# A gated cross-attention and feed-forward kernel: the order of the opening

## The chip, the cores and the metric

The kernel runs on one core of one Trainium2 chip. The metric is device microseconds of that core for one launch; lower is better. Three runs of the kernel before gave 1178.39, 1178.43 and 1180.54 us, so its median is 1178.43 us. A profiled execution of its own took 1179.06 us, and 1177.3 us of that is the span from the first instruction to the last.

The core has five engines that run their own instruction streams and meet only at semaphores: TensorE (PE; its weight loads are listed apart as PEld), VectorE (DVE), ScalarE (ACT), GpSimd (POOL) and SyncE (SP), which here only issues DMAs. All loads go through the queue of SP but one of 0.5 KB, which ACT issues.

## The reference, cut to what matters

```python
# x: (8, 224, 2048), ctx: (8, 750, 512), mask: (224, 750)
x = x + tanh(g_xattn) * attention(layernorm(x), ctx, ctx, mask)   # 32 heads of 64, 8 key/value heads
x = x + tanh(g_ffn) * gated_ffn(layernorm(x), weights...)         # router, top 8 of 512 slots, gate
# attention: softmax(q @ k.T / 8 + mask) @ v, where q is layernorm(x), k = v = ctx
```

The change lies wholly in the first 25 us: in the first layer norm of batch 0 and in what leads from it to the first attention products. Everything that is computed stays as it is.

## The kernel before, in words

**Tiles.** The 224 rows of a batch are cut in two. The first 128 are the top rows, one per partition, 2048 values each, in `xa[:, b]`. The other 96 are the rest: they are laid out so that each of 128 partitions holds, for 3 blocks (`NB = 3`), a quarter of a row (512 values), in `xb[:, b % 3]`. A partition thus knows only the mean and variance of its own quarter of each rest row, and four of them have to be joined.

**Units and windows.** The attention phase walks over 64 windows (8 batches by 8 key/value heads; `GROUPS`), and each window has 7 units (`UNITS`): 4 of top rows (one for each query head of the group) and 3 of the rest. Unit `n` takes 128 query rows against 750 context rows. Its path is: scores on PE (`score_main`, line 909, 512 columns, and `score_mid`, line 920, 238 columns, each twice because the keys are split in a high and a low part), mask and maximum on DVE (line 1303, which writes `neg_max`), exponential on ACT (line 723), transposition on PE (`turn_main`, line 932, and `turn_mid`, line 939), evacuation on ACT (line 719), the low part of the split on POOL (line 590), and the value products on PE (`value`, lines 956, 957 and 962; line 962 alone needs POOL's low part). Each engine's loop has one step `k` per unit, from `FIRST = -14` on, and every stage works at its own distance: in step `k` PE turns unit `k + 2`, scores unit `k + 5` and multiplies the values of unit `k`; DVE takes the maximum of `k + 4`; ACT takes the exponential of `k + 4`; POOL splits `k + 2`. The order within a step is written out by hand, and each engine works strictly in that order.

**Keys and values.** Two sets of buffers take turns. SP loads the keys of window `w + 2` when all 7 units of window `w` are scored (`load_k`, line 412, two DMAs of 187.5 KB each, one for each half of the partitions), and the values when POOL has split the ones of window `w + 1` (`load_v`, line 415). POOL splits the keys of window `w + 2` (`split_k`, line 557) in step 5 of window `w`, ahead of the low parts of the units that follow.

**The opening.** SP issues its loads without waiting, one after the other: top rows of batch 0 (1024 KB), the rest rows (768 KB), keys 0, the first mask (375 KB), values 0, the other masks (1125 KB), keys 1, values 1, top and rest rows of batch 1, then the feed-forward weights (four times 1024 KB, 512 KB, and small ones up to `in_log_rel`). DVE runs `top_stats(0, 0..3)` (line 1174) when the top rows are there, merges them (line 1187), and then `rest_stats` (line 1181). POOL makes the scale and bias from the top rows' numbers (lines 536 to 551), ACT normalizes the first 512 columns (line 687), PE transposes two of their blocks (`turn_first(0)`, line 887), ACT rounds them to bf16 (line 703, `round_first`), DVE writes the low parts (line 1200, `split_first`), and the scores of unit 0 begin.

**The rest rows' variance** is joined by two tiny products of PE with the matrix `quad`: the mean (line 1006) and, after three small DVE steps (lines 1220 to 1224), the variance (line 1024). DVE copies the result (line 1227), and this copy stands ahead of the DVE loop and so ahead of the first maximum. It releases `rest_joined`, on which POOL waits (line 536) before it makes the factors of the rest rows and normalizes them (line 583: three pieces for `rest_first`, three for `rest_widened`). From these PE transposes the query blocks of the rest rows of pair 0: `turn_first(1)` in step -3 and `turn_first(2)` in step -2. The first unit's transposition is `turn_main(0)` in step -2, so behind `turn_first(1)` in PE's order. ACT's `round_first(1)` has the same place in step -3.

Of the kernel before, what the change touches and what calls it, by code (L numbers as in the profile page):

```python
# [20 lines left out]
NB = REST // QUAD  # L21
# [48 lines left out]
def flamingo_block(nc, x_top, x_rest, k_t, v_rows, mask, g_x, av_t, wvd_t, w1_t, wq_t, wr, wr_rows_in, keys_t, log_rel, rel, b1, w2, wvu_t,  # L70
                   scalars, spill, out):
    with ExitStack() as ctx:
# [6 lines left out]
        def sem(name):  # L79
            return ctx.enter_context(nc.semaphore(name))  # L80
# [168 lines left out]
        top_normed = sem("top_normed")  # L249
        rest_normed = sem("rest_normed")  # L250
        rest_first = sem("rest_first")
        top_second = sem("top_second")
        spilled = [sem(f"spilled{i}") for i in range(3)]
        k_loaded = [sem("k_loaded0"), sem("k_loaded1")]
# [148 lines left out]
        def _(sp):  # L403
# [3 lines left out]
            def load_top(b):  # L407
                sp.dma_start(xa[:, b, :], x_top[b]).then_inc(top_loaded[b], 16)
# [23 lines left out]
                        sp.dma_start(spill[at:at + QUAD].rearrange("i (g r d) -> i g r d", g=KV, r=REP)[:, :, r, :],  # L432
                                     xb[QUAD * r:QUAD * r + QUAD, b % 3, j].rearrange("i (g d) -> i g d", g=KV)).then_inc(spilled[b % 3], 16)

            load_top(0)
            load_rest(0)
            load_k(0)
            sp.dma_start(mask_sb[:, 0:1, :], mask[:, 0:1, :]).then_inc(mask_loaded, 16)
# [240 lines left out]
        def _(act):  # L679
# [34 lines left out]
            for k in range(FIRST, NU):  # L714
                window, m = place(k)
                n = k + 2
                if 0 <= n < NU and not evac_on_dve(n):
                    act.wait_ge(turned, n + 1)
                    act.activation(p_sb[:, n % RING, :], flat_ps[:, turned_at(n):turned_at(n) + CW], ACT.Copy).then_inc(evac_a, 1)  # L719
                n = k + 4  # L720
                if 0 <= n < NU:
                    act.wait_ge(maxed, n + 1)
                    act.activation(s_sb[:, n % RING, 0:CTX], s_sb[:, n % RING, 0:CTX], ACT.Exp, bias=neg_max[:, n % 4, :],  # L723
                                   scale=-1.0).then_inc(exped, 1)
                g = window + 1
                if m == 0 and 0 <= g < GROUPS:
                    act.wait_ge(v_loaded[g % 2], 16 * (g // 2 + 1))
                    if g >= 2:
                        act.wait_ge(valued, UNITS * (g - 1))
                    else:  # L730
                        act.wait_ge(v_ones_set, 1)
                    act.activation(v_hi[:, g % 2, :, 0:D], v_raw[:, g % 2], ACT.Copy).then_inc(v_hi_done, 1)
                pair = window // 2 + 1
                if m == 4 and 1 <= pair < PAIRS:
                    act.wait_ge(q_turned, window + 4)
                if k in (-3, -2):
                    round_first(k + 4)
                later = (window - 3) // KV + 1
                if m == 6 and window >= 1:
                    if window % KV in (1, 2):  # L740
                        norm_top(4 * (window // KV) + 1 + window % KV)
                    elif later < BATCH and window % KV == 3:
                        norm_top(4 * later)
                    elif later < BATCH and window % KV in (4, 5, 6):
                        norm_rest(later, window % KV - 4)
                    elif later < BATCH and window % KV == 7:
                        norm_top(4 * later + 1)
                if window == 2 and m == 2:
                    act.wait_ge(small_loaded, 80)
                    act.activation(tanh_gf[:, :], scal[:, 0:1], ACT.Tanh).then_inc(gf_tanh, 1)  # L750
                    act.activation(keys_hi[:, :], keys_raw, ACT.Copy, scale=float(BOT) ** -0.5).then_inc(keys_hi_done, 1)
                if window == 3 and m == 2:
                    act.wait_ge(weights_loaded, 16)
                    act.activation(wq_cat[:, :, 0:BOT], wq_raw, ACT.Copy).then_inc(wq_hi_done, 1)
                if k in (NU - 4, NU - 3):
                    round_h(0, k - (NU - 4))
# [95 lines left out]
        def _(pe):  # L852
# [154 lines left out]
            for k in range(FIRST, NU):  # L1007
                window, m = place(k)
                if 0 <= k + 2 < NU:
                    turn_main(k + 2)  # L1010
                    turn_mid(k + 2)
                if 0 <= k + 5 < NU:
                    score_main(k + 5)
                if k >= 0:
                    value(k)
                if k in (NU - 4, NU - 3):
                    turn_h(0, k - (NU - 4))
                if k == NU - 2:
                    sum_wide(0, 0)
                if 0 <= k + 5 < NU:  # L1020
                    score_mid(k + 5)
                if k + 5 == 0:
                    pe.wait_ge(own_step, 3)
                    pe.matmul(psum[:, 3, 0:NB], quad[:, :], own_sum[:, :], start=True, stop=True).then_inc(own_spread, 1)
                if m == 2 and 1 <= window // 2 + 1 < PAIRS:
                    turn_q(window)
                if k in (-3, -2):
                    turn_first(k + 4)

            def sum_v2(pieces):  # L1030
                for i in pieces:
# [134 lines left out]
        def _(dve):  # L1166
# [2 lines left out]
            dve.memset(rk_aug[:, :], 0.0).then_inc(pads_set, 1)  # L1169

            def top_stats(b, c):
                if c == 0:
                    dve.wait_ge(top_loaded[b], 16)
                ins = dve.bn_stats(stats_top[:, c, :], xa[:, b, 512 * c:512 * c + 512])
                if c == 3:
                    ins.then_inc(top_summed, 1)
# [46 lines left out]
            dve.wait_ge(own_step, 2)  # L1223
            dve.tensor_tensor(own_sum[:, :], own_sq[:, :], own_mv[:, :, 1], ALU.add).then_inc(own_step, 1)
            dve.tensor_copy(ln_mv[:, 1:1 + NB, 0], psum[:, 5, 0:NB])
            dve.wait_ge(own_spread, 1)
            dve.tensor_copy(ln_mv[:, 1:1 + NB, 1], psum[:, 3, 0:NB]).then_inc(rest_joined, 1)
            dve.wait_ge(mask_loaded, 16)
            dve.wait_ge(gx_tanh, 1)

# [65 lines left out]
            for k in range(FIRST, NU + TO_CLOSE):  # L1296
                window, m = place(k)
                n = k + 4
                if n == REP:
                    dve.wait_ge(mask_rest_loaded, 16)  # L1300
                if 0 <= n < NU:
                    dve.wait_ge(scored, n + 1)
                    dve.tensor_tensor_reduce(s_sb[:, n % RING, 0:CTX], flat_ps[:, score_at(n):score_at(n) + CTX],  # L1303
                                             mask_sb[:, max(n % UNITS - REP + 1, 0), :],
                                             -1.0, 3.4e38, ALU.add, ALU.min, neg_max[:, n % 4, :]).then_inc(maxed, 1)
                n = k + 2
                if 0 <= n < NU and evac_on_dve(n):
                    dve.wait_ge(turned, n + 1)
                    dve.tensor_copy(p_sb[:, n % RING, :], flat_ps[:, turned_at(n):turned_at(n) + CW]).then_inc(evac_v, 1)
                if m == 0 and window >= 1:  # L1310
                    add_part(window - 1, range(0, 3))
                if m == 1 and window >= 1:
                    add_part(window - 1, range(3, UNITS))
                pair = window // 2 + 1
                if m == 3 and 1 <= pair < PAIRS:
                    turns = turn_range(window)
                    dve.wait_ge(q_turned, window + 4)
                    for half in range(2):
                        dve.tensor_copy(q_t[D * half:D * half + D, pair % 2, half, turns[0]:turns[-1] + 1, :],
                                        mix_ps[D * half:D * half + D, (window + 1) % 2, 0:128 * len(turns)].rearrange("p (t n) -> p t n", n=128)  # L1320
                                        ).then_inc(q_hi_own, 1)
                if m in (4, 5) and 1 <= pair < PAIRS:
                    split_q((window + 1) % 2, pair, m - 4, turn_range(window), 2 * (window + 3) + m - 4 + 1)
                if k in (-2, -1):
                    split_first(k + 3)
                next_stats(window, m)
                b = window // KV + 1
                if 0 <= window < GROUPS and b < BATCH:
                    if window % KV == 2 and m == 2:
                        merge_top(b)  # L1330
                        merge_rest(b)
                if m == 2 and EARLY_AT <= window < EARLY_AT + 4 * EARLY:
                    u, c = divmod(window - EARLY_AT, 4)
                    if c == 0:
                        dve.wait_ge(x_added, KV * (u + 1))
                        if u >= 1:
                            dve.wait_ge(mv2_done, u)
                    bank_stats(u, c)
                    if c == 3:
                        merge2(u)  # L1340
                if k == NU - 5:
                    stage_h(0, 0)
                    stage_h(0, 1)
                if k in (NU - 3, NU - 2):
                    split_h(0, k - (NU - 3))
                    stage_h(0, k - (NU - 3) + 2)
# [221 lines left out]
```

## Time and profile before

| | us |
|---|---|
| median of three runs | 1178.43 |
| profiled execution | 1179.06 |
| its span | 1177.3 |
| PE busy | 1139.6 (97% of the span) |
| DVE busy | 944.6 (80%) |
| ACT busy | 916.7 (78%) |
| POOL busy | 889.9 (76%) |
| top rows of batch 0: issue to landing | 5.9 |
| first value product on PE begins at | 24.84 |

The profile is one execution. Its times are in us from the start of the span. The views used are the page's busy times, the chain of waits (what the last instruction was waiting for, followed back), the timeline (instructions in order of time, alike ones merged), the waits, the DMA issues with their time to landing, and busy times by stretch. A wait is put down to what ended last before it.

### The profile page before, as it was taken

What the parts mean: (1) busy time and instruction counts of PE and PEld (TensorE: products, weight loads), DVE (VectorE), ACT (ScalarE), POOL (GpSimd) and SP (SyncE); (2) the same over time, 40 slices, a digit from 0 to 9 for tenths busy, and PEclk for the clock granted to TensorE, in tenths of its full rate; (3) what the DMA queues carried; (4) which work ended last, traced back from release to release, by engine and by line L of the source; (5) the groups of instructions that cost most, each with busy time, mean ns of one, the idle gap of its engine ahead of it and who ended that gap; (6) DMA issues with size and microseconds to landing.
All of it is one profiled execution on the core that took longest, in us unless ns stands there. A gap on an engine that the chain in (4) does not pass through costs nothing.

```text
span 1177.3 us, 35064 instructions
## 1 busy us (share of the span) xinstructions
PE 1139.6 (97%) x14385; PEld 913.8 (78%) x14642; DVE 944.6 (80%) x2255; ACT 916.7 (78%) x1226; POOL 889.9 (76%) x804
## 2 busy tenths in 40 slices
PE   5999999999999999999999999999999999999997
PEld 3888888888888888888888888888887665555554
DVE  5988888888888888888888888888874899676765
ACT  5899898888998898998899988999881444555544
POOL 6899999999999999999999999999991110404222
PEclk9999999999999999999999999999999999999999
DMA  9421231132114212311321131121225500011224
GB/s 336 148 69 48 57 116 45 52 83 97 42 42 116 70 48 57 115 49 48 86 93 42 46 78 49 42 58 51 62 87 182 209 2 1 1 68 77 107 99 152
DMA packets 60735, 95.09 MB, mean 81 GB/s; under 512 B 35233, under 2 KB 44449, under 8 KB 56482
## 3 DMA queue, kind: packets, MB, share of 16 engines
q1 hardware_dynamic: 59858, 91.79, 25.4%
q8 instruction: 118, 1.93, 0.7%
q10 hardware_dynamic: 720, 1.05, 0.3%
q14 instruction: 39, 0.32, 0.1%
HBM read 71.75 MB, written 20.97 MB: 79 GB/s over the span
## 4 chain that ended last, share of the span: by engine, by line
PE 73%; POOL 20%; DMA 2%; issue 2%; DVE 2%; SPq 1%; ACT 0%; DVEq 0%; POOLq 0%
POOL arena L590 14%; PE psum L985 12%; PE psum L932 12%; PE psum L909 11%; PE psum L939 6%; PE psum L920 6%; PE psum L962 5%; PE psum L956 5%; PE psum L957 5%; PE psum L1066 3%; POOL arena L557 2%; PE psum L972 2%; PE psum L999 2%; PE psum L887 2%; POOL arena L610 1%
## 5 line engine op out<-in xcount | busy, mean ns | idle before, releaser
L590 POOL TENSOR_TENSOR arena<-arena 128x768 bf16<-128x768 f32 x448 | 651.8, 1470 | 40.2 <-ACT arena L719 37.6
L1303 DVE CUSTOM_DVE_ANT_0 arena<-psum,arena 128x750 f32<-128x750 f32 x448 | 420.5, 939 | 127.4 <-PE psum L920 121.9
L719 ACT ACTIVATE arena<-psum 128x768 f32<-128x768 f32 x448 | 362.2, 809 | 89.4 <-PE psum L939 89.3
L723 ACT ACTIVATE arena<-arena,neg_max 128x750 f32<-128x750 f32 x448 | 410.9, 917 | 3.8 <-DVE neg_max L1303 3.7
L932 PE MATMUL psum<-ident,arena 128*128 128x128 f32 x1792 | 268.8, 273 | 0.0
L956 PEld LDWEIGHTS psum<-arena 128*128 128x128 bf16 (+1 forms) x2688 | 194.7, 98 | 57.6
L909 PE MATMUL psum<-arena 128*128 128x512 bf16 x674 | 222.5, 384 | 14.9 <-DVE arena L1200 0.8
L957 PE MATMUL psum<-arena 128*128 128x64 bf16 (+1 forms) x2688 | 222.2, 193 | 0.0
L956 PE MATMUL psum<-arena 128*128 128x65 bf16 (+1 forms) x2688 | 221.9, 194 | 0.0
L957 PEld LDWEIGHTS psum<-arena 128*128 128x128 bf16 (+1 forms) x2688 | 178.5, 98 | 53.2
L932 PEld LDWEIGHTS psum<-ident,arena 128*128 128x128 f32 x1792 | 206.7, 140 | 4.3
L939 PE MATMUL psum<-ident,arena 128*128 128x128 f32 x896 | 171.5, 273 | 0.2 <-ACT arena L719 0.2
L920 PE MATMUL psum<-arena 128*128 128x238 bf16 x896 | 167.5, 268 | 0.9 <-DVE neg_max L1303 0.9
L962 PE MATMUL psum<-arena 128*128 128x65 bf16 (+1 forms) x2688 | 160.1, 194 | 1.3 <-POOL arena L590 1.3
L985 PE MATMUL psum<-arena 128*128 128x512 bf16 x648 | 156.8, 384 | 1.5
L985 PEld LDWEIGHTS psum<-arena 128*128 128x128 bf16 x672 | 63.6, 96 | 75.0 <-issue 0.8
L962 PEld LDWEIGHTS psum<-arena 128*128 128x128 bf16 (+1 forms) x2688 | 114.9, 98 | 1.9 <-POOL arena L590 1.9
L939 PEld LDWEIGHTS psum<-ident,arena 128*128 128x128 f32 x896 | 112.2, 141 | 0.5 <-ACT arena L719 0.4
L699 ACT ACTIVATE arena<-psum 128x512 bf16<-128x512 f32 x56 | 33.3, 597 | 96.2 <-PE psum L972 96.2
L1246 DVE SCALAR_TENSOR_TENSOR arena<-psum,r_den,arena 128x64 f32<-128x64 f32 x448 | 97.5, 278 | 2.3
L557 POOL TENSOR_TENSOR arena<-arena 128x750 bf16<-128x750 f32 x64 | 92.1, 1439 | 1.8 <-DMA arena<-in_k_t 1.8
L909 PEld LDWEIGHTS psum<-arena 128*128 128x128 bf16 x896 | 87.8, 98 | 6.1 <-issue 0.8
(161 smaller groups left out, 1267.1 us busy)
## 6 DMA issues: line engine op xcount, KB each, us to landing
arena<-in_k_t SPq DMA_DIRECT2D x128, 187.5 KB, 3.2
arena<-in_v_rows SPq DMA_DIRECT2D x64, 192.0 KB, 2.5
out<-arena SPq DMA_DIRECT2D x12, 1024.0 KB, 3.9
arena<-in_x_top SPq DMA_DIRECT2D x8, 1024.0 KB, 5.3
arena<-in_x_rest SPq DMA_DIRECT2D x8, 768.0 KB, 4.5
spill<-arena SPq DMA_DIRECT2D x96, 64.0 KB, 2.2
arena<-spill SPq DMA_DIRECT2D x6, 1024.0 KB, 10.6
arena<-in_w_t SPq DMA_DIRECT2D x4, 1024.0 KB, 19.9
```

The lines of the kernel that those rows point to most:

```text
L590: pool.tensor_tensor(p_lo[:, n % RING, :], p_sb[:, n % RING, :], high(p_sb[:, n % RING, :]), ALU.subtract).then_inc(p_split, 1)
L719: act.activation(p_sb[:, n % RING, :], flat_ps[:, turned_at(n):turned_at(n) + CW], ACT.Copy).then_inc(evac_a, 1)
L723: act.activation(s_sb[:, n % RING, 0:CTX], s_sb[:, n % RING, 0:CTX], ACT.Exp, bias=neg_max[:, n % 4, :], scale=-1.0).then_inc(exped, 1)
L909: pe.matmul(flat_ps[:, score_at(n) + cols.start:score_at(n) + cols.stop], q_t[:, pair % 2, half, turn, :], kk, start=(i == 0), stop=(i == 1))
L920: mm = pe.matmul(flat_ps[:, score_at(n) + cols.start:score_at(n) + cols.stop], q_t[:, g // 2 % 2, half, turn, :], kk, start=(i == 0), stop ...
L932: pe.transpose(flat_ps[:, at:at + 128], s_sb[:, n % RING, c * 128:(c + 1) * 128], ident[:, :])
L939: mm = pe.transpose(flat_ps[:, at:at + 128], s_sb[:, n % RING, c * 128:(c + 1) * 128], ident[:, :])
L956: pe.matmul(o, hi, v_hi[0:rows, u, c, :], start=(c == 0), stop=False, skip_group_check=True)
L957: pe.matmul(o[:, 0:D], hi, v_lo[0:rows, u, c, :], start=False, stop=False, skip_group_check=True)
L962: mm = pe.matmul(o, lo, v_hi[0:rows, u, c, :], start=False, stop=(c == NCH - 1), skip_group_check=True)
L985: mm = pe.matmul(psum[:, 2, :], h[:, j, kk, :], w, start=(k == 0 and n == 0), stop=(k == KC - 1 and n == 2))
L1303: dve.tensor_tensor_reduce(s_sb[:, n % RING, 0:CTX], flat_ps[:, score_at(n):score_at(n) + CTX], mask_sb[:, max(n % UNITS - REP + 1, 0), :] ...
```

## The change

Four things change place. The top rows of batch 0 are loaded by two DMAs of 1024 columns each, with a semaphore of its own for the first, and the first two `top_stats` wait only for that one. DVE's copy of the rest rows' variance moves from ahead of the loop to behind the maximum of unit 0. On PE, `turn_first(1)` moves from the end of step -3 to step -2, behind the transposition of unit 0 and ahead of `score_main(3)`. On ACT, `round_first(1)` moves likewise from step -3 to step -2, behind the evacuation of unit 0 and ahead of the exponential of unit 2.

```diff
+        top_first = sem("top_first")
...
-            load_top(0)
+            sp.dma_start(xa[:, 0, 0:HID // 2], x_top[0, :, 0:HID // 2]).then_inc(top_first, 16)
+            sp.dma_start(xa[:, 0, HID // 2:HID], x_top[0, :, HID // 2:HID]).then_inc(top_loaded[0], 16)
             load_rest(0)
...  ACT, in the loop
+                if k == -2:
+                    round_first(1)
                 n = k + 4
...
-                if k in (-3, -2):
-                    round_first(k + 4)
+                if k == -2:
+                    round_first(2)
...  PE, in the loop
                     turn_main(k + 2)
                     turn_mid(k + 2)
+                if k == -2:
+                    turn_first(1)
                 if 0 <= k + 5 < NU:
                     score_main(k + 5)
...
-                if k in (-3, -2):
-                    turn_first(k + 4)
+                if k == -2:
+                    turn_first(2)
...  DVE
             def top_stats(b, c):
-                if c == 0:
+                if b == 0 and c == 0:
+                    dve.wait_ge(top_first, 16)
+                if c == (2 if b == 0 else 0):
                     dve.wait_ge(top_loaded[b], 16)
...
             dve.tensor_copy(ln_mv[:, 1:1 + NB, 0], psum[:, 5, 0:NB])
-            dve.wait_ge(own_spread, 1)
-            dve.tensor_copy(ln_mv[:, 1:1 + NB, 1], psum[:, 3, 0:NB]).then_inc(rest_joined, 1)
...  DVE, in the loop, behind the maximum of unit n = k + 4
+                if n == 0:
+                    dve.wait_ge(own_spread, 1)
+                    dve.tensor_copy(ln_mv[:, 1:1 + NB, 1], psum[:, 3, 0:NB]).then_inc(rest_joined, 1)
```

## Rows read from the trace of the kernel before

**Rows 1.** The page, busy time, share of the span and instructions of each engine.
```profile
PE 1139.6 (97%) x14385; PEld 913.8 (78%) x14642; DVE 944.6 (80%) x2255; ACT 916.7 (78%) x1226; POOL 889.9 (76%) x804
```

**Rows 2.** The chain of waits, 0 to 60: start us, us, what.
```profile
0.72 5.91 DMA arena<-in_x_top
...
28.18 10.07 DMA arena<-in_k_t
38.32 1.44 POOL arena L557
39.76 1.43 POOL arena L590
41.24 0.37 PE psum L962 x6
```

**Rows 3.** Waits from 27 to 60: us in total, times, longest.
```profile
POOL arena L557 <- DMA arena<-in_k_t: 1.5, 1, 1.5
PE psum L962 <- POOL arena L590: 0.4, 1, 0.4
```

**Rows 4.** Timeline, all engines, 0 to 15.4: start, us, what [idle before].
```profile
6.65 2.47 DVE L1174 BATCH_NORM_STATS2 stats_top<-arena 128x6 f32<-128x512 f32 x4 [4.39 <-DMA arena<-in_x_top]
9.55 1.88 DVE L1181 BATCH_NORM_STATS2 stats_rest<-arena 128x6 f32<-128x512 f32 x3
11.16 1.44 POOL L557 TENSOR_TENSOR arena<-arena 128x750 bf16<-128x750 f32 x1 [0.26 <-DMA arena<-in_k_t]
11.47 0.32 DVE L1216 BATCH_NORM_AGGREGATE own_mv<-stats_rest 128x2 f32<-128x6 f32 x3
13.00 0.88 DVE L1200 TENSOR_TENSOR arena<-psum,arena 64x256 bf16<-64x256 f32 x2 [1.22 <-ACT arena L703]
13.56 1.01 PE L909 MATMUL psum<-arena 128*128 128x512 bf16 x2 [0.79 <-DVE arena L1200]
15.24 0.16 DVE L1227 COPY ln_mv<-psum 128x3 f32<-128x3 f32 x1 [0.72 <-PE psum L1024]
```

**Rows 5.** Timeline, all engines, 15.4 to 32, same columns.
```profile
15.40 0.94 DVE L1303 CUSTOM_DVE_ANT_0 arena<-psum,arena 128x750 f32<-128x750 f32 x1
...
17.30 3.24 POOL L583 TENSOR_SCALAR arena<-arena,ln_scale,ln_bias 128x128 f32<-128x128 f32 x6
18.76 0.87 PE L887 MATMUL psum<-ident,arena 128*128 128x128 f32 x3 [0.16 <-POOL arena L583]
19.43 1.06 PE L932 MATMUL psum<-ident,arena 128*128 128x128 f32 x4
24.12 0.44 PE L939 MATMUL psum<-ident,arena 128*128 128x128 f32 x2 [0.15 <-ACT arena L719]
24.93 5.75 POOL L590 TENSOR_TENSOR arena<-arena 128x768 bf16<-128x768 f32 x4
27.07 0.35 PE L962 MATMUL psum<-arena 128*128 128x65 bf16 x6
```

**Rows 6.** DMA issues in 1.1 to 1.3: KB each, us to landing.
```profile
arena<-in_x_rest SPq DMA_DIRECT2D x1, 768.0 KB, 8.4
```

**Rows 7.** DMA issued in 21.4 to 21.5, then in 31.5 to 31.7.
```profile
arena<-in_v_rows SPq DMA_DIRECT2D x1, 192.0 KB, 15.8
...
arena<-in_v_rows SPq DMA_DIRECT2D x1, 192.0 KB, 7.2
```

**Rows 8.** Busy by stretch: us, PE, PEld, DVE, ACT, POOL, PEclk, DMA share, GB/s.
```profile
0.50:1.50 1.00, 0.00 (x0) 0.00 (x0) 0.59 (x2) 0.33 (x1) 0.53 (x5) 1.00 0.00 0
1.50:2.00 0.50, 0.00 (x0) 0.00 (x0) 0.44 (x2) 0.50 (x1) 0.44 (x8) 1.00 1.39 213
2.00:6.00 4.00, 0.00 (x0) 0.00 (x0) 0.26 (x1) 0.45 (x1) 1.35 (x5) 1.00 0.83 254
16.00:26.00 10.00, 9.11 (x63) 6.22 (x64) 6.28 (x15) 7.81 (x12) 9.72 (x14) 1.00 1.02 406
31.00:36.00 5.00, 4.94 (x82) 4.44 (x80) 4.81 (x9) 4.45 (x6) 4.14 (x4) 1.00 1.06 289
37.00:38.50 1.50, 1.50 (x18) 1.14 (x15) 1.02 (x5) 1.25 (x3) 0.18 (x1) 1.00 0.10 37
```

**Rows 9.** DMA in 6.5 to 8, then in 31 to 32.3: packets and mean rate.
```profile
DMA packets 126, 0.61 MB, mean 404 GB/s; under 512 B 12, under 2 KB 12, under 8 KB 126
...
DMA packets 196, 0.51 MB, mean 390 GB/s; under 512 B 81, under 2 KB 81, under 8 KB 188
```

## The prediction

> **What bounds the kernel now.** I read the page's busy times first: PE is busy in 97% of the span [rows 1], so past the opening the time is PE's stream, and what an opening can give is only what moves the start of that stream and is not taken back later. So I followed the chain of waits. It begins as expected: the top rows' load, 0.72 to 6.63, then DVE's variances. But it holds a second anchor far behind the opening: the keys of window 2, a DMA from 28.18 that took 10.07 us and landed at 38.25; behind it POOL splits them (38.32, 1.44 us), makes one low part (39.76, 1.43 us), and only then can PE's line 962 run at 41.24 [rows 2]. The waits from 27 to 60 show the size: POOL idle 1.5 us for this load, PE idle 0.4 us behind POOL (0.39 in the timeline) [rows 3]. These 1.5 us of POOL and 0.4 us of PE say that without the load PE would have been at line 962 at 41.24 - 0.39 = 40.85.
>
> The question is therefore whether a faster opening also moves that landing. The stretches say no. From 16 to 26 the 16 DMA engines are busy at 1.02 and move 406 GB/s, from 31 to 36 still at 1.06, and only in 37 to 38.5 are they down to 0.10 [rows 8]: the weights of the feed-forward phase, all issued without a wait in the first 19 us, fill the queue until about 37. The loads around the keys land in the order of issue: values 2, issued at 21.42, at 21.42 + 15.8 = 37.2; keys 2, issued from 27.67, at 38.25; values 3, issued at 31.57, at 31.57 + 7.2 = 38.8 [rows 2, 7]. The steps of 1.05 and 0.55 us between them are those of a queue being emptied, by a few engines that lag behind the others, not of a latency counted from the issue. A load issued 1 us sooner into this backlog stays behind the same bytes. Its landing is fixed by the amount queued since the first load, whatever PE does.
>
> **The change part by part.**
>
> *Top rows in two halves.* The four variances take 2.47 us from 6.65 on [rows 4]. The load moves 254 GB/s in 2 to 6 [rows 8], after the first pieces by 2.0, so half of it (0.52 MB, 2.1 us) has come at about 4.2, landed by 4.5 to 5; the first two variances (1.24 us) then end before the second half lands, and only two remain: the top rows' numbers come 1.24 us sooner, as long as the second half still lands at 6.6. POOL's factors and ACT's normalization follow at the same distance, so `turn_first(0)` and the rounding come 1.24 us sooner. DVE's low part of the first query was at 13.00 and could now run at 11.76. DVE isn't earlier with the rest rows: these land at 1.17 + 8.4 = 9.57 [rows 6], just where it takes them now (9.55), so it is busy until 11.47 + 0.32 = 11.79 [rows 4], and this cover costs nothing more. But the first scores need the split keys too: keys 0 land just before 11.16 (POOL had waited 0.26 us for them) and are split at 12.60 [rows 4]. The 13.56 of PE's line 909 is 0.13 behind its release at 13.43 (half of DVE's 0.88 from 13.00), so it becomes 12.60 + 0.13 = 12.73: a gain of 0.83, not 1.24; the other 0.41 die on the keys.
>
> *Its price.* SP issues one DMA more, some 0.4 us, which every later issue of the opening is late by; the backlog hides it, since the rest rows are moved from about 6 on. If the cover were gone it would be 0.4 us on each landing. Pieces of 4 KB in place of 8 KB: the trace has 4 KB pieces at 31 to 32.3, 390 GB/s, against 406 for the larger ones [rows 8, 9]; for 1.05 MB that is 2.69 against 2.58 us, 0.1 us more. I take +0.1 us for every landing. The bounds are wide: below, the load might run at the 404 GB/s of 6.5 to 8 [rows 9] and not at 254, 1.5 us less on all landings; above, a 4 KB piece might take as long as an 8 KB one does in this stretch, 4.1 us (1.05 MB at 254 GB/s) more. I take the value next to the nearest row.
>
> *First maximum ahead of the copy.* The maximum of unit 0 starts at 15.40 behind the copy, which had waited 0.72 us for line 1024 [rows 4, 5]. Scores 0 will end at about 14.97 - 0.83 = 14.14, since `score_mid(0)` is two more products behind `score_main(0)` (14.97 is the end of its pair, 13.56 + 1.01 + 0.40); the maximum then runs 14.17 to 15.12, 1.2 us sooner. The variance product, right behind scores 0 on PE, ends at about 14.8, so behind the maximum the copy finds it done and runs 15.15 to 15.31. Waiting behind it on DVE is only the maximum of unit 1, whose scores come at 15.85. `rest_joined` thus comes at 15.31 against 15.40: POOL gains 0.1 us, no more. Were the keys late once more, the copy would slip with the maximum, and POOL with it.
>
> *Unit 0's transposition first.* PE did `turn_first(1)` at 18.76 (0.87 us, after 0.16 idle for POOL's line 583), and only then `turn_main(0)`, whose first row is at 19.43 (line 932) and, in the chain, from 19.64 on [rows 5]. With scores 1 and 2 some 1.15 us sooner, PE is through with them at 17.45 and turns unit 0 from there to 18.75. `turn_first(1)` needs the third piece of POOL's line 583, which ends at 18.63 now (17.30 + 1.33) [rows 5] and at 18.53 then: it starts at 18.75 without a wait and ends at 19.62, where it ends today. So the rest rows' queries come no later, the evacuation of unit 0 comes 2 us sooner, and ACT's order (evacuation, rounding, exponential of 2) brings the exponential about 1 us sooner. Behind that the steps of PE come 0.7 to 0.9 sooner; by ACT's chain the wait of line 939 at 24.12 [rows 5] ends 0.9 sooner, with the first value product.
>
> *POOL takes a part of this.* POOL works from 17.30 almost without a gap: busy 9.72 of 10 us in 16 to 26 [rows 8]. Its four low parts from 24.93 last 5.75 us, 1.44 each [rows 5], and they shift by 0.1 only. The second value product needs the first of these four (24.93 + 1.44 = 26.37, then 26.27) for its line 962, which runs at 27.07 today; with 0.06 of release it can come at 26.33 at the earliest. So PE's lead is cut to 27.07 - 26.33 = 0.74 us. Later units ask for less.
>
> *The sum.* Up to 40 us PE is 0.74 us ahead: it stands at line 962 at 40.85 - 0.74 = 40.11. The keys land at 38.25 + 0.1 = 38.35, POOL needs 1.44 + 1.43 + 0.05, PE goes on at 41.34. The stall grows from 0.39 to 1.23, and the lead is gone. Nothing of it survives elsewhere: at 41.24 POOL and DVE have emptied their work today too, and what follows is the same code from the same state. The span changes by +0.1. The profiled execution would be 1179.06 + 0.1 = 1179.2; it lies 0.63 above the median of the runs, so against that the forecast is 1178.43 + 0.1 = 1178.5 us.
>
> **The rivals.**
>
> A. *The lead survives.* Keys 2 would have to land early enough for POOL, by 40.11 - 2.92 - 0.07 = 37.1 or before, 1.1 us sooner. For it speaks that the tail of the queue is thin (37 GB/s in 37 to 38.5 [rows 8]), so that the last engines may lag by less in another execution, and that 254 GB/s in the first stretch leaves room. Against it stand the order and steps of the landings [rows 7]. Gain 0.74, and the 0.39 of today's stall on top: 1.13, so 1177.3. Part of it, 0.3 to 0.7, is likelier than all.
>
> B. *The second half costs a gap of its own, slower.* The first load is issued at 0.72, no byte moves up to 1.5, and the first ones do by 2.0 [rows 2, 8]: up to 1.3 us. If the second half started with such a gap, not behind the first without a break, it would land 1.3 us later, the variances would gain nothing, and every landing, keys 2 included, would come 1.3 us later: 1178.4 + 1.3 = 1179.7. It decides from the first 0.1 us of gap on, as the keys' landing is on the path. Against it: in 6.5 to 8, where the top rows' last and the rest rows' first pieces meet, the queue moves 404 GB/s with no break [rows 9].
> The Trainium skill, "DMA: Bandwidth & Descriptors", section "Anatomy of one DMA", puts a fixed 2 us beside the bytes of each DMA (a fit for GpSimd's path), and its "Bandwidth" section wants 1 MiB or more per DMA. Counted one behind the other this would be an estimate of 2 us more, 1180.4. By the row at the seam, which shows no such cost between queued loads, I give it little.
>
> C. *The change does not do what it says:* the first half's semaphore comes only with the second's, because pieces of both are in flight on all engines. Then the top rows' numbers come as today and the gain is 0.4 by the order of DVE and 0.2 by that of PE; the keys take it all the same, 1178.5.
>
> **How the numbers follow.** Forecast (the keys' landing takes the lead, landing moved by -0.2 to +0.4): 0.62. A: 0.20. B: 0.10, of which a tail of 0.03 goes beyond 1180.8. C: 0.05. The rest, 0.03, is for gains beyond A, up to 2.4 us, if the landings came 1.5 us sooner and keys 0 with them. The range takes A's full gain, B's price and the bounds of the forecast: 1177.0 to 1179.9, with some 0.12 left outside, for the spread of the runs (one of three was 2.1 us above the others) and for the bounds of the half loads. 0.2% of the time is 2.36 us, about what a measurement can tell here from no change. Faster by more than that needs the whole tail: 0.04. Slower: 0.05. Same: 0.91.
>
> **What would show it.** Right: DVE's first `top_stats` pair near 4.5 to 5 and its second at 6.6; line 909 first at about 12.7; the first maximum at 14.2 with the copy behind it; line 932 ahead of the three of line 887, at 17.5; the first value product at about 24.0; keys 2 landing at 38.2 to 38.5 though issued 0.7 sooner; POOL's wait for them at 2.2 to 2.4 us; PE's wait at line 962 at 1.1 to 1.3 us; everything behind 41.3 as before. Wrong: a landing of keys 2 that follows its issue (the wait stays at 1.5), or a lead at 24 us of more than 1 us, or a second half that lands later than 7.

## The result: slower by 0.3%, by 3.5 us

The changed kernel took 1182.26 us (median of 18 runs, 1180.75 to 1185.19), the kernel before 1178.74 (18 runs, 1178.35 to 1180.54): ratio 1.003, 95% interval 1.0023 to 1.0037. The forecast was 1178.5, and its range ended at 1179.9. The profiled execution took 1183.01 us, its span 1181.2 against 1177.3: 3.9 us more.

The chain of waits of the changed kernel (columns: start us, us, what) names the place (before: [rows 2]). Lines have moved by a few: 559, 592 and 966 are the 557, 590 and 962 of before.

```profile
29.83 12.51 DMA arena<-in_k_t
42.41 1.44 POOL arena L559
43.84 1.43 POOL arena L592
45.32 0.37 PE psum L966 x6
```

Its waits from 27 to 60 (us in total, times, longest), which answer to [rows 3]:

```profile
POOL arena L559 <- DMA arena<-in_k_t: 4.0, 1, 4.0
PE psum L966 <- POOL arena L592: 3.2, 2, 2.8
```

The anchor, the landing that PE has to wait for, is where the prediction had it. Keys 2 land at 42.34 and not at 38.25, +4.09; PE goes on at 45.32 and not at 41.24, +4.08; the span is 3.9 longer. PE waits 2.8 us for what it had waited 0.4 for. The other half of the forecast, that this landing stays where it was, is what failed. The timeline (start, us, what [idle before]) shows that the landings are late from the first load on, against [rows 4, 5]:

```profile
5.88 1.29 DVE L1182 BATCH_NORM_STATS2 stats_top<-arena 128x6 f32<-128x512 f32 x2 [3.62 <-DMA arena<-in_x_top]
7.82 1.29 DVE L1182 BATCH_NORM_STATS2 stats_top<-arena 128x6 f32<-128x512 f32 x2 [0.65 <-DMA arena<-in_x_top]
11.47 1.88 DVE L1189 BATCH_NORM_STATS2 stats_rest<-arena 128x6 f32<-128x512 f32 x3 [2.07 <-DMA arena<-in_x_rest]
13.52 1.44 POOL L559 TENSOR_TENSOR arena<-arena 128x750 bf16<-128x750 f32 x1 [2.65 <-DMA arena<-in_k_t]
15.02 1.03 PE L913 MATMUL psum<-arena 128*128 128x512 bf16 x2 [0.61 <-POOL arena L559]
16.64 0.94 DVE L1309 CUSTOM_DVE_ANT_0 arena<-psum,arena 128x750 f32<-128x750 f32 x1 [1.38 <-PE psum L924]
17.50 0.15 DVE L1314 COPY ln_mv<-psum 128x3 f32<-128x3 f32 x1
19.55 3.24 POOL L585 TENSOR_SCALAR arena<-arena,ln_scale,ln_bias 128x128 f32<-128x128 f32 x6
28.71 0.36 PE L966 MATMUL psum<-arena 128*128 128x65 bf16 x6 [0.40 <-POOL arena L592]
```

The second half of the top rows lands at 7.8, where the whole load had landed at 6.6; the rest rows at 11.4 (9.57), keys 0 at 13.5 (11.1). So the scores start 1.46 us later and not 0.83 sooner, POOL's chain 2.25 later, the second value product 1.64 later. The busy times by stretch (columns as in [rows 8]) show how the queue lost it:

```profile
2.00:6.00 4.00, 0.00 (x0) 0.00 (x0) 0.38 (x2) 0.45 (x1) 1.35 (x5) 1.00 0.81 197
8.00:11.00 3.00, 0.00 (x0) 0.00 (x0) 1.37 (x3) 0.09 (x1) 1.14 (x4) 1.00 1.08 209
16.00:20.00 4.00, 3.73 (x15) 1.72 (x13) 2.09 (x6) 1.68 (x2) 1.89 (x6) 1.00 1.03 212
```

The kernel before, in the last two of these stretches:

```profile
8.00:11.00 3.00, 0.00 (x0) 0.00 (x0) 2.84 (x6) 0.07 (x1) 1.14 (x4) 1.00 1.02 237
16.00:20.00 4.00, 3.33 (x13) 1.83 (x13) 2.25 (x6) 2.17 (x3) 3.72 (x9) 1.00 1.03 380
```

The DMA engines are about as busy as before (0.81 for 0.83 in 2 to 6 [rows 8], 1.03 for 1.03 in 16 to 20), but move fewer bytes: 197 for 254 GB/s in 2 to 6. The pair of 16 to 20, 212 for 380, is of different loads. Added up from the start, 3.9 MB have moved by 14.0 in the kernel before and 4.0 MB by 16.0 in the changed one, and with that keys 1 are next in the queue. The kernel before has its own slow stretch there, of 3 us:

```profile
14.00:15.00 1.00, 1.00 (x6) 0.66 (x5) 0.46 (x4) 0.00 (x0) 0.00 (x0) 1.00 1.04 246
15.00:16.00 1.00, 1.00 (x3) 0.17 (x3) 0.76 (x2) 0.00 (x0) 0.42 (x2) 1.00 1.00 227
16.00:17.00 1.00, 0.67 (x4) 0.43 (x4) 0.35 (x2) 0.61 (x1) 0.84 (x3) 1.00 1.07 267
17.00:18.00 1.00, 0.84 (x2) 0.00 (x0) 0.95 (x2) 0.31 (x1) 0.88 (x3) 1.00 1.06 429
```

In the changed kernel the slow stretch is all of 16 to 20. That makes two questions: what slows the start, and what turns 1.2 us at the top rows into 4.1 at keys 2.

### The profile page after: what moved, and what is told of

Same layout as the page of the kernel before. It is cut to its first block, busy times and chain, and to the rows that moved or that the text cites. A ratio compares the mean times of both kernels' runs of the same rounds, so it can differ in the third digit from the quotient of the medians.

```text
span 1181.2 us, 35322 instructions
## 1 busy us (share of the span) xinstructions
PE 1155.4 (98%) x14642; PEld 913.4 (77%) x14642; DVE 944.5 (80%) x2255; ACT 917.0 (78%) x1226; POOL 889.8 (75%) x804
## 4 chain that ended last, share of the span: by engine, by line
PE 74%; POOL 20%; DMA 3%; DVE 1%; issue 1%; SPq 1%; ACT 0%; DVEq 0%; POOLq 0%
POOL arena L592 14%; PE psum L989 12%; PE psum L913 12%; PE psum L936 12%; PE psum L943 6%; PE psum L924 6%; PE psum L966 5%; PE psum L960 5%; PE psum L961 5%; PE psum L1072 3%; POOL arena L559 2%; PE psum L1003 2%; DMA arena<-in_k_t 2%; PE psum L976 2%; PE psum L891 1%; POOL arena L612 1%
## 5 line engine op out<-in xcount | busy, mean ns | idle before, releaser
L913 PE MATMUL psum<-arena 128*128 128x512 bf16 x896 | 272.3, 385 | 0.6 <-POOL arena L559 0.6
L989 PE MATMUL psum<-arena 128*128 128x512 bf16 x672 | 161.2, 384 | 0.0
```

The lines of the kernel that those rows point to most:

```text
L913: pe.matmul(flat_ps[:, score_at(n) + cols.start:score_at(n) + cols.stop], q_t[:, pair % 2, half, turn, :], kk, start=(i == 0), stop=(i == 1))
L989: mm = pe.matmul(psum[:, 2, :], h[:, j, kk, :], w, start=(k == 0 and n == 0), stop=(k == KC - 1 and n == 2))
```

## The experiments

All ran against the kernel before on the same chip (its median 1178.5 to 1178.9 there).

**Which part of the change.** e1 is the kernel before with only the load and DVE's waits for it, e2 the changed kernel with one load.

```diff
 e1:  -load_top(0)
      +sp.dma_start(xa[:, 0, 0:HID // 2], ...).then_inc(top_first, 16)
      +sp.dma_start(xa[:, 0, HID // 2:HID], ...).then_inc(top_loaded[0], 16)
 e2:  the same lines the other way, in the changed kernel
```

> The kernel before with only the top rows' load in two halves (and DVE's waits for them); all orders on DVE, ACT and PE as before. Theory L (the load is the cause, the orders are not): keys 2 land near 42.3 as in the changed kernel and the time is +3.5 us, 1182.2 (1181 to 1184). Rival O (the new orders, above all the copy behind the first maximum, cost the time): keys 2 land at 38.3 and the time is within 0.5 us of before, 1178.7.

> The changed kernel with the top rows in one load again: only the orders of DVE, ACT and PE are new. Theory L: keys 2 land at 38.25 and PE's lead is taken there; time as before, 1178.7 (1178.3 to 1179.0), with PE's first value product some 0.5 us sooner and POOL's wait for keys 2 some 0.5 us longer. Rival O: +2 to +3.5 us, 1181 to 1182.

e1: 1183.83 us (6 runs), ratio 1.0037, 1.0024 to 1.005, keys 2 landing at 41.67. e2: 1178.73, ratio 0.9994, 0.997 to 1.0019, keys 2 landing at 38.87 (38.25 expected). The load is the whole loss, the orders give nothing measurable. In e2 two lines of the trace count:

```profile
16.09 0.15 DVE L1310 COPY ln_mv<-psum 128x3 f32<-128x3 f32 x1
27.30 0.24 PEld L964 LDWEIGHTS psum<-arena 128*128 128x128 bf16 x6 [0.25 <-POOL arena L590]
```

With one load the scores start about when they did before, and the copy behind the first maximum runs at 16.09 and not 15.24. So POOL starts on the rest rows about 0.85 later, and the second value product waits for POOL and stands at 27.30 (27.07 before [rows 5]). The lead of 0.5 us that I had expected of PE does not exist: the first value product starts at 24.79 (24.84 before), the second 0.23 later than before.

**The pieces of the second queue.** The gate (`g_x`, 128 values) is loaded on ACT's queue in the same microsecond, as 128 pieces of 4 bytes. e3 and e4 take this load off: e3 from the changed kernel, e4 from the kernel before.

```diff
 ACT: -act.dma_start(tanh_gx[:, :], g_x).then_inc(gx_loaded, 16)      # and its wait and tanh
      +act.activation(warm[:, :], ones[:, 0:1], ACT.Tanh)             # keeps the table's load where it was
 SP, behind load_v(0):
      +sp.dma_start(tanh_gx[:, :], g_x).then_inc(gx_loaded, 16)
 ACT, step 0:  the wait and the tanh;  DVE's wait for it: ahead of the first add_part
```

> The changed kernel with the load of the gate (128 pieces of 4 bytes) taken from ACT's queue at the start to SP's queue behind values 0, its tanh in ACT's step 0. Theory T (each piece of the top rows that alternates with a tiny piece of the other queue takes about 0.4 us whatever its size, so halving the pieces halves what moves in that time): with no tiny pieces the first half lands by 4.3, the second by 5.3, keys 2 at 37 or sooner, and the time falls under that of before: 1177.5 (1176.8 to 1178.3). Rival P (4 KB pieces or one DMA more are slow by themselves or set the DMA engines out of step): the second half lands at 7 or later, keys 2 at 41 or later, time 1181 or more.

> The kernel before with the same move of the gate's load and tanh. Theory T: 8 pieces an engine run at the 404 GB/s of 6.5 to 8 and not at 254, the top rows land at 5.2 and not 6.6, everything of the opening and keys 2 come 1.3 to 1.5 us sooner, and PE's stall at keys 2 stays at 0.4: 1177.3 (1176.8 to 1178.0). Rival P: the start is slow whatever the second queue does, no change: 1178.7.

e3: 1178.27 (ratio 0.9995, 0.9987 to 1.0004). e4: 1178.30 (0.9994, 0.9986 to 1.0003). Four microseconds of the changed kernel go with 128 pieces of 4 bytes. The kernel before gets 0.5 us from it and not the 1.3 to 1.5 that I had expected, and its interval does not tell even this from nothing: its first load lands 0.97 sooner (5.66), but keys 2 only 0.53 sooner (37.72), and PE waits 1.4 us there. The DMA view of 2 to 4 (packets of each queue, MB, share of 16 engines; q1 is SP's, q10 ACT's) in the kernel before, then the changed kernel, e3 and e4:

```profile
q1 hardware_dynamic: 64, 0.52, 79.6%
q10 hardware_dynamic: 61, 0.00, 1.7%
```
```profile
q1 hardware_dynamic: 79, 0.32, 82.8%
q10 hardware_dynamic: 64, 0.00, 1.7%
```
```profile
q1 hardware_dynamic: 142, 0.53, 82.8%
```
```profile
q1 hardware_dynamic: 69, 0.57, 70.6%
```

Beside 64 large pieces in 2 us go 61 tiny ones; beside 79 in the changed kernel, 64. These are the counts of two queues that take turns, nearly piece by piece. From the same lines (share of 16 engines, times 2 us, over the pieces) an 8 KB piece took 0.40 us beside the tiny ones and 0.33 without them, a 4 KB piece 0.34 and 0.19. So while the queues take turns, half the bytes take most of the time of the whole: little more than the same number of pieces moves 0.32 MB and not 0.52. With the tiny pieces gone 142 pieces of 4 KB pass, 0.53 MB. The Trainium skill, "DMA: Bandwidth & Descriptors", section "Queues, rings and completion order", says that each DMA engine goes round its queues packet by packet; the trace agrees closely for the 8 KB pieces, 64 to 61, and less closely for those of 4 KB, 79 to 64.

The split is not free without the tiny pieces either. DVE gets the rest rows at 9.35 in e3 and has them by 8.52 in e4, and keys 2 land at 38.03 and 37.72. The two medians are the same.

**Doubling it.** e10 issues the gate's load twice on ACT's queue in the kernel before.

> The kernel before with the gate's load issued twice on ACT's queue (the second into a spare tile), so 18 tiny pieces an engine instead of 9; the top rows in one load. Theory T: the alternation goes on beyond the top rows into the rest rows and the first keys, the rest rows land 1 us later or more, keys 2 near 39.5 or later, and the time is +1.3 us or more: 1180.1 (1179.6 to 1182). Rival P (only size and number of the top rows' loads matter): as before, 1178.8.

1178.95 (ratio 1.0001, 0.9992 to 1.001): not slower. 6 to 8 fell from 395 to 304 GB/s, but 8 to 11 rose from 237 to 284, the rest rows were there when DVE asked for them at 9.46, and keys 0 at 11.1 as before. So bytes that are late at one place are not always late at the next. My theory that every turn costs a fixed time, whatever else is going on, falls; what holds is the measured effect on the first 4 KB pieces. Why the stretch of the keys makes up for a later round of turns is open.

**One more load and 4 KB pieces, with no second queue.** e11 splits the top rows of batch 1 in the same way, in the kernel before.

> The kernel before with the top rows of batch 1 (issued near 6.8, when no other queue has work) in two halves, those of batch 0 in one. It has the same two things, one DMA more and 4 KB pieces, without the alternation. Theory T: keys 2 within 0.3 us of 38.25, time as before, 1178.8 (within 0.4). Rival P: keys 2 at 40 or later, 1181 or more.

1178.71 (ratio 1.0, 0.9991 to 1.0009), keys 2 being split from 38.19 on (38.32 before). Neither the second DMA nor the piece size costs anything there.

**How much is the anchor.** e6 (from the changed kernel) and e9 (from the kernel before) issue the five large weight loads behind keys 2.

```diff
-for i in range(4): sp.dma_start(w1_raw[...], w1_t[i])...
-sp.dma_start(wq_raw, wq_t).then_inc(weights_loaded, 16)
 ...
                     load_k(window + 2)
+                if window == 0:
+                    (the same five loads)
```

> The changed kernel with the five large loads of the feed-forward weights issued behind keys 2 instead of in the opening. It parts what the opening itself lost from what the keys' landing took. Theory N (two losses, of which only the later one counts at the end): the opening is as late as in the changed kernel (second value product's line 966 at 28.7, 1.64 us behind before), keys 2 land long before they are needed, and the time is 1178.8 + 1.64 - 0.39 = 1180.0 (1179.3 to 1180.7), so 2 to 3 us of the loss go. Rival: the landing of keys 2 costs nothing that the opening hadn't lost, 1182 to 1183.

> The kernel before with the five weight loads behind keys 2. Theory N: only the stall of 0.39 us at keys 2 goes, 1178.4 (1178.1 to 1178.8). Rival: the weights collide with what is loaded later (keys 3, rows of batch 2) and it is slower, 1179.5 or more.

e6: 1179.78 (ratio 1.001, 1.0001 to 1.0019), e9: 1178.59 (0.9997, 0.9988 to 1.0006). In neither does POOL wait for keys 2. So of the loss of 3.5 us, 2.5 (1182.26 against 1179.78) go with the late landing of keys 2, and 1.0 to 1.2 are the late opening itself, which the wait for that landing hides in the changed kernel. That this landing holds PE up is shown; in the kernel before it costs too little to measure.

**What multiplies the lateness.** The keys are loaded by two DMAs that each write 64 partitions and read the same bytes. e12 (from the kernel before) and e13 (from the changed one) load them by one DMA to all 128, from an array that holds them twice. So three things change together: the number of DMAs, the partitions that each one writes, and where the second copy is read.

```diff
-for part in range(2):
-    sp.dma_start(k_raw[D * part:D * part + D, g % 2, :], k_t[g]).then_inc(k_loaded[g % 2], 16)
+sp.dma_start(k_raw[:, g % 2, :], k_t[g]).then_inc(k_loaded[g % 2], 16)
 ...  and POOL waits for 16 per load and not 32
```

> The kernel before with each window's keys loaded by one DMA to all 128 partitions (the array in memory holds them twice) and not by two DMAs to 64 partitions each. Theory H (a load that writes only half of the partitions moves at half the rate, 200 GB/s in 8 to 11 against 400 for the others): the stretch 8 to 11 moves 330 GB/s or more, keys 0 land 0.9 us sooner, keys 2 some 2 us sooner (36 to 36.7), the stall of 0.39 us goes, 1178.4 (1178.0 to 1178.7); PE's start stays, since it waits for the first query. Rival: the rate comes from pieces of 3000 bytes, no change in 8 to 11, 1178.8.

> The changed kernel with the keys loaded by one DMA to all 128 partitions. Theory S (the split load puts the DMA engines out of step, and engines out of step hinder each other most at the half-partition key loads, which turns 1.2 us at the top rows into 4.1 us at keys 2): keys 2 land by 39, and the time is 1180.0 (1179.3 to 1180.6), as when the weights came later. Rival R (the later part of the loss has nothing to do with the keys' loads): keys 2 at 40.3 to 41.3, only the 1 to 2 us sooner that the faster loads give the kernel before too, 1181 or more.

e12: 1178.09 (ratio 0.9992, 0.9983 to 1.0001). e13: 1178.25 (0.9996, 0.9987 to 1.0005), 4.0 us less than the changed kernel, 0.2 over e12, and 1.75 less than I had expected. Its runs lie in 0.85 us (1178.0 to 1178.85), those of the changed kernel in 4.4. By stretch in e12, then e13:

```profile
8.00:11.00 3.00, 0.00 (x0) 0.00 (x0) 2.97 (x6) 0.03 (x1) 1.21 (x5) 1.00 1.05 423
16.00:20.00 4.00, 2.84 (x17) 1.68 (x17) 2.40 (x7) 2.46 (x4) 3.73 (x9) 1.00 1.01 418
```
```profile
8.00:11.00 3.00, 0.00 (x0) 0.00 (x0) 2.65 (x6) 0.21 (x1) 1.38 (x5) 1.00 1.07 425
16.00:20.00 4.00, 3.79 (x17) 2.33 (x18) 1.94 (x5) 2.40 (x3) 3.51 (x9) 1.00 1.01 418
```

And e13's timeline:

```profile
7.70 1.29 DVE L1181 BATCH_NORM_STATS2 stats_top<-arena 128x6 f32<-128x512 f32 x2 [0.33 <-DMA arena<-in_x_top]
9.60 1.88 DVE L1188 BATCH_NORM_STATS2 stats_rest<-arena 128x6 f32<-128x512 f32 x3 [0.31 <-DMA arena<-in_x_rest]
36.76 1.44 POOL L558 TENSOR_TENSOR arena<-arena 128x750 bf16<-128x750 f32 x1
```

Here the second half of the top rows is nearly as late as in the changed kernel (7.7 for 7.8), but the rest rows come at 9.6 and not 11.47, and POOL finds keys 2 there. So the first microsecond goes with the alternation, and nearly all that grows out of it went with the keys' two loads. I counted in the records when the first and the last of the 128 pieces of the rest rows start, and when the first piece of keys 0 starts, in us from the first piece of all (v2 and v5, further down, have no tiny pieces; v5 has the keys by one DMA):

```
                first   last    between   keys 0 from
before          3.74    6.42    2.68      5.85
changed         4.18    8.20    4.02      6.03
e1              4.13    8.20    4.07      5.98
e13             4.01    7.19    3.18      5.86
e3              3.25    6.37    3.12      5.16
v2              3.16    7.54    4.38      5.09
v5              3.26    5.74    2.48      5.11
```

In the changed kernel the last pieces of the rest rows start 2.2 us behind the first of the keys, in the kernel before 0.6, in e13 1.3. I read this as DMA engines that have drifted apart, so that some are at the keys while others are still at the rest rows, and hinder each other there; the records don't name the engine of a piece, so this is inferred. The 256 pieces of 3000 bytes of keys 0 and the first mask take 0.19 us each in the kernel before, 0.23 in the changed one and 0.12 in e12 and e13 (medians), so their size is not what makes them slow. That it is the writes to one half of the partitions, and not the second DMA or the second reading of the same bytes, is not shown. And the drift needs no second queue: v2 has the widest spread of all without one. What turns the split into a drift is open.

**Versions without the alternation.** v1: the kernel before with the gate's load moved and the weights late. v2: that and the top rows in halves. v5: that and keys by one DMA. v6: v5 with the changed kernel's orders. v7: v5 with the weights in the opening again.

> The kernel before, its orders and its one load of the top rows, with the gate's load on SP's queue and the weights behind keys 2. With the gate's load moved the second value product's line 966 had come at 25.49, 1.58 us sooner than before, and keys 2 had taken 1.43 + the rest of it; with the weights out of the way both should stay: 1178.8 - 1.58 - 0.39 = 1176.8 (1176.4 to 1177.3). If later loads have another anchor, 1178 or more.

> As the last one, with the top rows in two halves (DVE's waits for them too), the orders of DVE, PE and ACT as before. The halves now land without alternation; the top rows' numbers were at 7.93 with them and at 8.46 without. PE's first scores then wait for the keys (12.5 against 12.6) and POOL's chain for the rest rows: 0 to 0.3 us sooner than the last one, 1176.6 (1176.0 to 1177.2). Rival: the halves cost 0.3 us or more of the landings of rest rows and keys, and it is slower than the last one by 0.3 or more.

> Top rows in halves, gate's load on SP's queue, keys by one DMA to 128 partitions, weights behind keys 2; orders of before. Theory: nothing of the queue is late now; the top rows' numbers come at 7.9 or sooner, rest rows by 8.8, keys 0 by 9.6; PE's first scores, bound by the first query, at 11.9 to 12.2; 0.3 to 0.8 us under the version with two key loads: 1175.9 (1175.4 to 1176.5). Rival: DVE or POOL sets the pace of the opening and the keys give nothing, 1176.4 or more.

> The same loads, with the changed kernel's orders (first maximum ahead of the variance's copy, unit 0's transposition ahead of the rest rows' queries). Theory Q (the copy behind the first maximum delays POOL's chain for the rest rows, and the second value product waits for POOL): 0.2 to 0.5 us slower than with the old orders, 1176.3. Rival G (with early landings the new orders gain what the prediction gave them, 0.2 to 0.7 us): 1175.4 or less.

> As the first of these, with the weights in the opening again. Theory: with the keys at full rate the whole backlog is emptied near 34 to 35 and keys 2 land before POOL asks for them (35.3 to 35.7), so the weights' place costs nothing: within 0.3 us of it, 1176.0. Rival: keys 2 land at 36.5 or later, POOL waits and it is 1 us slower, 1176.9.

| | median us | ratio to before, 95% |
|---|---|---|
| v1 | 1177.14 | 0.9986 (0.9977 to 0.9995) |
| v2 | 1176.43 | 0.9982 (0.9974 to 0.9991) |
| v5 | 1176.28 | 0.9979 (0.9971 to 0.9988) |
| v6 | 1176.73 | 0.9984 (0.9975 to 0.9992) |
| v7 | 1176.09 | 0.9979 (0.9970 to 0.9987) |

v7 beats both kernels, by 2.4 and 6.2 us, and needs no other place for the weights: with the keys at full rate POOL's wait for keys 2 is 0.3 us and reaches nobody. Once nothing alternates the halves are worth 0.7 us (v1 to v2) and the new orders cost 0.45 (v5 to v6); in both cases the intervals overlap. v2's profile is of its slowest run (1178.32), with the second half of the top rows at 7.1 and the rest rows at 10.2: halves with keys in two loads can still drift, with no second queue. For the new orders the timelines say where the time would go. v5, then v6:

```profile
13.58 0.16 DVE L1235 COPY ln_mv<-psum 128x3 f32<-128x3 f32 x1 [0.72 <-PE psum L1030]
15.64 3.24 POOL L587 TENSOR_SCALAR arena<-arena,ln_scale,ln_bias 128x128 f32<-128x128 f32 x6
```
```profile
14.25 0.16 DVE L1317 COPY ln_mv<-psum 128x3 f32<-128x3 f32 x1
16.30 3.24 POOL L587 TENSOR_SCALAR arena<-arena,ln_scale,ln_bias 128x128 f32<-128x128 f32 x6
```

The scores start at 11.90 and 11.81. In v6 the first maximum is 0.32 sooner (13.39 for 13.71), but the copy 0.67 later, and POOL with it (16.30 for 15.64).

## Why the prediction was wrong

- **The anchor at keys 2: right.** The prediction had PE's lead or lag decided by this landing, and the landing set by the backlog and not by the issue. The landing moved 4.09 us and PE's restart 4.08, while the issue of the keys moved 1.65 (29.32 for 27.67).
- **The failed step: the price of two halves.** I took +0.1 us for every landing, from 4 KB pieces at 31 to 32.3 [rows 9], where no second queue was at work. It measured +1.2 at the top rows and +4.1 at keys 2. My upper bound was that a 4 KB piece takes as long as one of 8 KB in this stretch, 4.1 us more. That comes near to what happens while the queues alternate (0.34 for 0.40 us in 2 to 4), but only for a part of the pieces, and that its size is the one measured at keys 2 is chance: two thirds came later, in the stretches of the rest rows and keys. I named this bound and then gave it almost no weight, although it came from the very stretch in question: 254 GB/s in 2 to 6 against 404 in 6.5 to 8 should have been explained first. The tiny pieces were a part of what made it slow: without them (e4) 2 to 4 moved 283 GB/s for 262, and 4 to 6 moved 410 for 246. Beside them the split cost most.
- **The top rows' numbers 1.24 sooner: wrong.** They came at the same time (DVE's merge at 9.14 for 9.16), since the second half was 1.2 late. With nothing alternating, all four variances follow each other from 5.14 on in e3 and from 4.95 on in v5, though not in v2's profiled run.
- **`rest_joined` at 15.31: wrong by 2.3 us** (copy ends 17.65). Nearly all of it is the start of the scores, 15.02 for the predicted 12.73; from there on the chain was right to 0.05 us. The prediction said that late keys would make the copy slip with the maximum, and POOL with it. This happened, and e2 shows more: with the scores where they were before (13.62 for 13.56), the copy's new place alone puts POOL off by about 0.85.
- **PE's order:** line 936 did run ahead of the three of line 891 (19.63 and 21.01), but PE then waited 0.31 us for POOL's third piece. The prediction let PE's steps come 0.7 to 0.9 us sooner with early scores, and its rival C gave the new orders 0.6 us without them; e2 shows none of that at the first value product, and v5 and v6 suggest a small loss with the copy's place.
- **Rival B** had the right sign and place (a late second half puts off every landing), with the wrong mechanism (a gap ahead of it) and a third of the price. The range ended at 1179.9 since no rival let a delay grow behind the load where it arose.

## What to carry to other kernels

Before a load is cut, ask what else is in flight in that stretch: here the smaller pieces lost against another queue's tiny ones, as the queues took turns by pieces and not by bytes. Look for a stretch where the DMA engines are busy and the bytes are few (here 1.02 busy, 237 GB/s), and for data that is loaded once for each half of the partitions: in this kernel, with one DMA for all 128, the same stretch moved 423 GB/s. Where an engine waits for the end of a backlog, follow a delay at its head through every load up to there. It can grow on the way (1.2 us became 4.1) or vanish (e10, e13), and a gain can shrink (e4: 0.97 us at the first load, 0.53 at keys 2).

## What the runs showed of the hardware that I had not expected

- 128 pieces of 4 bytes on a second queue cost the first load of 1 MB about 1 us (landing at 5.66 without them, 6.63 with), and 4 us of the changed kernel's time.
- The same 128 pieces again, right behind the first, cost nothing (e10: 1178.95 for 1178.7).
- With the keys in two loads to 64 partitions each, the stretch of keys 0 (8 to 11) moved 237 GB/s, with all engines busy; with one load to 128, 423.
- Taking away either the tiny pieces (e3) or the keys' second load (e13) gave back 4.0 us. Neither shows alone what makes the loads drift: v2 drifted without the tiny pieces.
